# Chunks of 125 tokens, two chunks of edges per bucket and a joint stage without GpSimd in a graph transformer kernel

## The reference

```python
# L0: embedding, 4 hops over the graph, linear attention, 2 of 8 experts
xn = layernorm(x)
x1 = xn @ W1 + b1                       # 1250x512
out = x1
for k in range(4):
    deg = segment_sum(ones, dst); dis = maximum(deg, 1) ** -0.5
    alpha = tanh(out[dst] @ gw[k][:512] + out[src] @ gw[k][512:] + gb[k])
    out = out + segment_sum((dis[src] * dis[dst])[:, None] * alpha * out[src], dst)
x = x + concat([x1, out], 1) + attention0(xn) @ Wo.T + bo
x = x + experts(layernorm(x))           # the two best of 8 by a gate
# L1: a sparse linear layer built from the same edges, attention, gated MLP
xn = layernorm(x)
W = zeros(1024, 1024).at[row, col].add(nnz_weight)   # row=src, col=dst, edge_weight;
x = x + xn @ W.T + bias + attention1(xn) @ Wo1.T + bo1   # indices past 1023 are dropped
x = x + mlp(layernorm(x))
```

## Time and profile before

| | |
|---|---|
| median of 3 runs | 2728.61 us (2726.71 to 2731.57) |
| the profiled execution | 2738.93 us |
| its span | 2736.9 us |
| TensorE matmul | 2291.4 us (84%) |
| VectorE | 1724.4 us (63%) |
| ScalarE | 1007.2 us (37%) |
| GpSimd | 384.8 us (14%) |
| DMA, moved | 253.43 MB, 93 GB/s on average |

### The profile page before, as it was taken

The page is one execution under the profiler, slowest core; times in us unless marked ns, Lnnn a source line. Parts: engine busy times, 40 slices in busy tenths (PEclk is TensorE's granted clock), DMA queues, the critical chain, the costliest instruction groups (busy, mean ns, idle before and its releaser), DMA issues. The chain is left out here.

```text
span 2736.9 us, 33962 instructions
## 1 busy us (share of the span) xinstructions
PE 2291.4 (84%) x12790; PEld 2012.8 (74%) x12790; DVE 1724.4 (63%) x2712; ACT 1007.2 (37%) x1551; POOL 384.8 (14%) x332
## 2 busy tenths in 40 slices
PE   0689999994885699996279999994979999989798
PEld 0669999993663577775268888883759999977697
DVE  8865656656887877775279999995653333335422
ACT  0512322222442344441068888884112222221120
POOL 0257750002771000000200000001100000000000
PEclk9899999997998799996589999997999999999999
DMA  0252211103232000005655445514421111124314
GB/s 17 75 175 51 47 37 40 64 12 134 92 107 88 8 1 8 8 1 183 232 191 179 169 165 197 185 47 176 145 104 60 35 60 45 37 82 140 113 64 127
DMA packets 100988, 253.43 MB, mean 93 GB/s; under 512 B 16507, under 2 KB 43506, under 8 KB 100822
## 3 DMA queue, kind: packets, MB, share of 16 engines
q1 hardware_dynamic: 90006, 230.24, 24.0%
q0 software_dynamic: 10816, 20.99, 2.7%
HBM read 289.28 MB, written 81.27 MB: 135 GB/s over the span
## 5 line engine op out<-in xcount | busy, mean ns | idle before, releaser
L1945 DVE TENSOR_TENSOR ex_wl<-ex_raw,ex_wh 128x1024 fp32r<-128x1024 f32 x324 | 376.0, 1222 | 58.9 <-ACT ex_wh L2012 58.4
L2012 ACT ACTIVATE ex_wh<-ex_raw 128x1024 fp32r<-128x1024 f32 x324 | 329.6, 1059 | 94.3 <-DMA ex_raw<-in_experts 57.6
L1284 DVE TENSOR_TENSOR m_kvf<-m_bank,m_bkv 128x256 f32<-128x256 f32 (+1 forms) x160 | 67.9, 425 | 228.7 <-PE m_bank L1189 218.0
L953 POOL DMA_INDIRECT scratch_slots<-pay,idx x160 | 196.7, 1229 | 59.6 <-issue 59.6
L1434 PE MATMUL gl_bank<-gl_gh,gl_al 128*128 128x512 f32 (+3 forms) x400 | 164.6, 412 | 29.5 <-DVE g L1513 18.3
L1189 PE MATMUL m_bank<-m_w_lo,xh 128*128 128x256 f32 (+1 forms) x1280 | 178.4, 282 | 0.0
L1189 PE MATMUL m_bank<-m_w_hi,xl 128*128 128x256 f32 (+1 forms) x1280 | 177.5, 281 | 0.2 <-issue 0.2
L1189 PE MATMUL m_bank<-m_w_hi,xh 128*128 128x256 f32 (+1 forms) x1280 | 177.2, 281 | 0.0
L1189 PEld LDWEIGHTS m_bank<-m_w_lo,xh 128*128 128x128 f32 (+1 forms) x1280 | 163.9, 186 | 0.1
L1189 PEld LDWEIGHTS m_bank<-m_w_hi,xl 128*128 128x128 f32 (+1 forms) x1280 | 162.4, 186 | 0.6 <-issue 0.6
L1189 PEld LDWEIGHTS m_bank<-m_w_hi,xh 128*128 128x128 f32 (+1 forms) x1280 | 161.5, 186 | 0.2 <-issue 0.2
(11 more groups left out here) (396 smaller groups left out, 5527.2 us busy)
## 6 DMA issues: line engine op xcount, KB each, us to landing
ex_raw<-in_experts SPq DMA_DIRECT2D x324, 512.0 KB
m_w_raw<-in_qkv SPq DMA_DIRECT2D x48, 512.0 KB
ex_xr<-scratch_seats SPq DMA_DIRECT2D x27, 512.0 KB, 3.5
scratch_served<-ex_y SPq DMA_DIRECT2D x27, 512.0 KB, 2.6
scratch_at<-m_ats SPq DMA_DIRECT2D x48, 209.0 KB
o_ar<-scratch_at SPq DMA_DIRECT2D x18, 512.0 KB
o_xr<-scratch_res SPq DMA_DIRECT2D x18, 512.0 KB
scratch_res<-o_xr SPq DMA_DIRECT2D x18, 512.0 KB
```

Of the source, the lines that this page charges most:

```text
L953: e.indirect_dma_start(dram["slot_rows"], bass.IndirectOffsetOnAxis(idx[:, k:k + 1].bitcast(U32), 0), pay[:, k, :], None).then_inc(scat.se ...
L1284: e.tensor_tensor(f, bank[KVB + s % 3][0:r, 0:W2], bkv[0:r], ALU.add)
L1945: return e.tensor_tensor(wl[:, n % RING], raw[:, unit[1]], wh[:, n % RING].bitcast(F32), ALU.subtract)
L2012: e.activation(wh[:, n % RING], raw[:, unit[1]], ACT.Copy).then_inc(high.sem)
```

## The change

All chunks have `TP` = 125 tokens, ten of them. The chunk of an index is found by a multiplication with 1049 and a shift by 17. A bucket has two columns of 128 places (`HOME` = 2), so 200 columns of slots and not 300. In the given data a bucket holds 200 edges on average and 248 at most. The buckets are ordered by target first. `wmat` is a matrix of 1125x1125 in its natural layout, built from nine (`WB`) blocks each way.

```diff
-LAST = N - (TC - 1) * P
+TP = N // TC
-HOME = 3
+WB = -(-D // TP)
+HOME = 2
 def rows_of(c):
-    return P if c < TC - 1 else LAST
+    return TP
 def tokens(c):
-    return slice(c * P, c * P + rows_of(c))
+    return slice(c * TP, (c + 1) * TP)
```

In `graph_sort` the one-hot has 16-bit operands, four wide at the inside:

```diff
-            e.tensor_tensor(hot[:], key[:].unsqueeze(1).broadcast_to([EP, NBUCK, EK]),
-                            iob[0:EP, :].unsqueeze(2).broadcast_to([EP, NBUCK, EK]), ALU.is_equal)
+            by4 = lambda t: t.rearrange("p b (k f) -> p b k f", f=4)
+            e.tensor_tensor(by4(hot[:]), by4(keyb[:].unsqueeze(1).broadcast_to([EP, NBUCK, EK])),
+                            iob[0:EP].unsqueeze(2).broadcast_to([EP, NBUCK, EK // 4, 4]), ALU.is_equal)
```

```diff
         @block.gpsimd
-            e.wait_ge(*parted["wlo"])
-            for n, (i, q) in enumerate(groups):
-                if q == 0:
...
-                    e.tensor_tensor(t, t, bias[0:rows_of(i)], ALU.add).then_inc(based.sem)
-                if (i, q) in scaled.value:
...
-                    e.tensor_tensor(ws[:, r, HOME:HC, 0], hs[:, r, HOME:HC],
-                                    wide(whi[:, cut(i, q, HOME, HOME)].bitcast(F32), HOME), ALU.mult)
-                    e.tensor_tensor(ws[:, r, :, 1], hs[:, r], wide(wlo[:, cut(i, q)], HC),
-                                    ALU.mult).then_inc(scaled_pl.sem)
         @block.scalar
+            for n, (i, h) in enumerate(groups):
+                if h == 0 and i + 1 < TC:
+                    split_at(i + 1)
+                g = groups[n + 1] if n + 1 < len(groups) and groups[n + 1] in kept else None
+                if g:
+                    make_real(g)
+                note((i, h, 0))
+                if g:
+                    scale(g, 0, UN // 2)
+                note((i, h, 2))
+                if g:
+                    scale(g, UN // 2, UN)
+                note((i, h, 4))
         @block.vector
             def hot(n):
-                col = iot[:].unsqueeze(1).broadcast_to([P, HC, P])
-                e.tensor_tensor(hs[:, r], wide(slots[:, cut(i, q), 0], HC), col, ALU.is_equal).then_inc(source.sem)
-                e.tensor_tensor(hd[:, r], wide(slots[:, cut(i, q), 1], HC), col, ALU.is_equal).then_inc(target.sem)
+                by4 = lambda t: t.rearrange("p u (k f) -> p u k f", f=4)
+                col = by4(iot[:].unsqueeze(1).broadcast_to([P, UN, P]))
+                for t4, t, sem in ((s4, hs, source), (d4, hd, target)):
+                    val = t4[:, first(g):first(g) + UN].unsqueeze(2).broadcast_to([P, UN, P // 4, 4])
+                    e.tensor_tensor(by4(t[:, n % HOT]), col, val, ALU.is_equal).then_inc(sem.sem)
+            for n, (i, h) in enumerate(groups):
+                if h == 0 and i + 1 < TC:
+                    split_at(i + 1)
+                if n + 2 < len(groups):
+                    hot(n + 2)
+                if n + 1 < len(groups):
+                    low(n + 1)
+                add((i, h, 0))
+                if h == 0:
+                    rebase(i)
+                add((i, h, 2))
+                if h == 0 and i:
+                    evict(i - 1)
+                add((i, h, 4))
```

More of the change, by code:

```diff
@@ L525, in project_and_count @@
         x_out = [p.raises(f"x_out{b}", range(b, TC, 3), 16) for b in range(3)]
[L526 to L531, removed]
@@ L532, in project_and_count @@
-        stored = [p.raises(f"stored{b}", range(b, KC, 2), 16) for b in range(2)]
+        s_in, b_in, consts = p.raises("s_in", ["slots"], 16), p.raises("b_in", ["bias"], 16), p.raises("consts", ["iota"])
+        at_high, at_low, based, done, summed = (p.raises(n_, C) for n_ in ("at_high", "at_low", "based", "done", "summed"))
+        fours, parted = p.raises("fours", ["source", "target"]), p.raises("parted", ["wlo"])
+        source, target = p.raises("source", groups), p.raises("target", groups)
@@ L547, in project_and_count, with first @@
         block = p.block()
-        def cut(i, q, first=0, count=HC):
-            at_ = (i * TC + q * GW) * HOME + first
-            return slice(at_, at_ + count)
+        def first(g):
+            return (g[0] * TC + g[1] * HB) * HOME
         @block.sync
@@ L614, in _, with count @@
         @block.tensor
         def _(e):
-            def count(n):
-                g, b, r = groups[n], n % 2, n % RING
-                e.wait_ge(*cast[g])
+            def count(sub):
+                i, h, f = sub
+                g, n = (i, h), nth[sub]
+                b, r = n % 2, turn[g] % HOT
+                if f == 0:
+                    e.wait_ge(*target[g])
                 if n >= 2:
-                    e.wait_ge(*noted[groups[n - 2]])
-                for d in range(GW):
+                    e.wait_ge(*noted[subs[n - 2]])
+                for d in range(blocks(*sub, TC)):
@@ new lines, in scale, with note @@
+            def scale(g, from_, to):
+                n = kept[g]
+                for u in range(from_, to):
+                    c = first(g) + u
+                    a = e.activation(ws[:, n % EVEN, u, 0], hs[:, turn[g] % HOT, u, 0:TP], ACT.Copy,
+                                     scale=whi[:, c:c + 1].bitcast(F32))
+                if to == UN:
+                    a.then_inc(scaled.sem)
+            def note(sub):
+                i, h, f = sub
+                nb = blocks(*sub, TC)
+                e.wait_ge(*counted[sub])
+                e.activation(c16[0:TP, h * HB + f:h * HB + f + nb, tokens(i)], pc[nth[sub] % 2][0:TP, 0:nb, 0:TP],
@@ new lines, in _ @@
+            for u in range(4, KC):
+                w.make_high(e, u)
+            e.wait_ge(*parted["wlo"])
+            scale(groups[0], 0, UN)
+            for n, (i, h) in enumerate(groups):
[11 more added lines that the diff above has]
+                note((i, h, 4))
@@ L729, in _ @@
-            e.wait_ge(*ld["bias"])
+                e.tensor_tensor(t, t, py[c % 2][0:TP], ALU.add).then_inc(summed.sem)
+            e.wait_ge(*s_in["slots"])
             e.tensor_copy(whi[:], slots[:, :, 2])
@@ L1396, in _ @@
             for t in range(NT):
[L1397 removed]
+                m = e.matmul(bank[4 + t][:, 0:TW], ones[0:TP], ab[0:TP, tile(t)], start=True, stop=True)
             m.then_inc(row.sem)
```

342 lines of the change are left out of this document (180 added, 162 removed).

## The result

The changed kernel takes 2894.51 us (median of 4 runs, 2891.36 to 2898.59) against 2728.62 us: a ratio of 1.061, 95% interval 1.0597 to 1.0623. It is slower, as forecast, but by 166 us and not by 85, and the time lies outside the range of 2762 to 2852. The profiled execution took 2896.7 us with a span of 2895.0.

The account below looks back on a forecast made before the run. No engine bounds it throughout: waited-for transfers bound embedding, routing and the last stage; engines disturbing each other slow the joint stage. Terms -3+40-46+1.5+37+10+6+40 = +85.5 gave a median of 2814 us, range 2762 to 2852.

Parts of the forecast that it names:

- the transfer terms: All stages' added time from SyncE's 125-row tiles on five DMA engines: +134.5 us in all.
- The price of a 125-row transfer: SyncE's 125x1024 tile runs on 5 of 16 engines: 4.20 us against 1.34, so 2.86 more each.
- The first rival: 4 KB tiles spread over most engines, so transfer terms vanish: -49 us, 2680; chance 0.08.
- Transfers that GpSimd issues by an index list: GpSimd's indexed transfers were taken to be unlike SyncE's 125-row ones and costed at nothing.
- The last stage: Final load-and-store rounds grow from 5.55 to 10.6 us: +40 us (30 to 46).
- Embedding: Embedding's waiting rounds grow from 6.13 to 12 to 13.3 us, ending near 238: +40 us (28 to 46).
- Routing: Routing's six rounds grow from 5.6 to 9.9 to 11.3 us: +37 us (24 to 44).
- Serving: Three tiles now stand ahead of weights 4 to 7, plus a last store: +10 us (2 to 14).
- Joint stage: Weight-block period falls from 21.00 to 16.5 us, set by TensorE: -46 us (-33 to -56).
- The sort: Its 16000-element one-hot gets cheaper with 16-bit operands, less 1.2 for scalings and waits: -3 us (-7 to +1).
- The rest: Graph layer +1.5 (0 to 4), serving +10, second projection +6 (0 to 8), attention and experts 0.
- two rivals: Joint stage doesn't speed up, 2846 us, chance 0.13; half of embedding and routing is hidden, 2764, chance 0.10.

Follow-up runs that it names:

- the run with direct tiles on 16 engines: Changed kernel with SyncE's token tiles and sparse-weight block rows each moved as 112 and 13 rows; ratio 0.9909 to the kernel before.
- the kernel with both edits: Changed kernel with SyncE's tiles split into 112 and 13 rows and GpSimd's indexed tiles padded to 128 rows; 2663.60 us, ratio 0.9758 to the kernel before.

## Why the prediction was right and wrong

Over the whole kernel the sum splits so: giving the transfers their engines back is worth 231 us, where the transfer terms were 134.5; what is left of the change gains 65 us, where the sort and the joint stage were 49. That leaves 97 - 16 = 81 us, the distance from 85 to 166. Two steps failed: indexed transfers had no price, and the terms of the direct ones were too small, above all the joint stage's, which was nothing.

- **The price of a 125-row transfer: right.** Five engines, read from a DMA share of 0.33; the changed kernel shows 0.33 for a 4 KB tile (4.00 us, 112 GB/s), the cut into 96 and 29 rows shows the rule at its other end, and 112 and 13 rows take the price away. The first rival (4 KB rows spread over most engines, 2680) fell.
- **"Transfers that GpSimd issues by an index list are not of this kind and I cost them at nothing": the first of the two steps that failed.** The 40 of them in routing and serving cost 50 us. The changed kernel without this cost stands at a ratio of 1.0426, 2845 us on the first chip, which is inside the range. A sign was in the profile before, among GpSimd's groups, though it can be read only afterwards, since the transfers differ in bytes too: the edge scatters of 125 rows took 1229 ns each to issue and the indexed stores of 128 rows 955. In the changed kernel these take 1186. The groups of before, and of after:

```profile
L953 POOL DMA_INDIRECT scratch_slots<-pay,idx x160 | 196.7, 1229 | 59.6 <-issue 59.6
...
L1704 POOL DMA_INDIRECT scratch_seats<-ro_xn,seat x20 | 19.1, 955 | 83.6 <-DVE seat L1817 77.8 <-issue 5.8
```

```profile
L1760 POOL DMA_INDIRECT scratch_seats<-ro_xn,seat x20 | 23.7, 1186 | 128.9 <-DVE seat L1873 123.1 <-issue 5.8
```

- **The direct terms: 134.5 forecast, 201 measured by the stages (191 by the ratios): the second.** Taken from the run with direct tiles on 16 engines, what was missing is 19 us in the joint stage, 13 in the embedding, 12 in routing, 11 in serving, 7 in the last stage and 4 in the rest.
- **The last stage: right in kind, a little short.** Rounds of 11.04 us, near the upper of my two ends (11.3) and not the 10.6 between them: the fixed part stayed. The chain of waits is DMA for 82% of the stretch, as named; the share is 0.27 and not 0.31. +45.5 for +40, its upper bound 46.
- **Embedding: +53.4 for +40 (bound 46).** Rounds of 13.0 us where I had 12 to 13.3, but the tail was missing: the next phase begins at 245.2, when the last stores, issued from 230.0 on and sharing five engines, have landed. The stage ended 7 us later than the 238 named. (Its lower bound of +28 was a slip: 113.2 + 105 is 218, and 225 is 26.5 above 198.5.)
- **Routing: direct part +49.1 for +37, and the indexed 29 on top.** Six rounds of 10.87 us from 1273.48 to 1338.67; I took 10.5 and subtracted for a backlog.
- **Serving: +34.9 for +10 (bound 14).** 20.8 direct, 19.8 indexed, not quite additive. SyncE issues the first of weights 4 to 7 at 1962.28, 14.4 us after the phase's start at 1947.85, where it did so after 7.2 before (1885.13, 1877.93): the head had to wait for the first weights too, and I had counted only the three tiles ahead of the later ones. That the first weights are late because they share engines with a token tile and with the first gathers is likely, and not shown.
- **Joint stage: -41.5 for -46, a near hit by errors that cancel.** Its arithmetic gained 60.8 us. TensorE's period is 14.7 and not 16.4, because my price of a group took the whole time from 729.87 to 731.41, with its gaps, and scaled it by two thirds, 1.05. Without waits, in the kernel with both edits, four counts and four weight matmuls take 0.75 us:

```profile
713.25 0.39 PE L631 MATMUL o_pc<-o_hd,o_hs 128*125 128x125 bf16 x4
713.46 0.71 PE L645 MATMUL o_pw<-o_ws,o_hr 128*125 128x250 f32 x4
714.00 0.63 PE L229 MATMUL o_py<-o_w_lo,o_xh 128*125 128x512 f32 x2
```

  VectorE works about 12 us a chunk and not 16.1 (60.06 of 74), mostly because its 16-bit one-hots take 0.82 us and not 1.58. So the DMA became the bound, which I had put at 15.1, under 16.4, and which therefore had no term: it cost 19 us. Its 15.1 was itself added up wrong (10.5 is the embedding's sum, with a 512-column store that this stage doesn't have; two tiles and the weight's store make 13.0 by the same prices), and it had no fixed parts and no order. SyncE's rows show the order: the next load waits at 787.70 for the store issued at 775.08. The weight blocks' stores lie 17.3 us apart here, (793.69 - 759.04) / 2, two periods since short and long ones alternate. Over all eight intervals they lie 16.5 apart, (843.45 - 711.24) / 8, which is the number that I named, by luck: the first two are 13.3 and 14.7, before the tiles' transfers fall behind.

```profile
759.04 0.25 SPq L591 DMA_DIRECT2D scratch_wmat<-o_wacc  x1
...
775.08 0.40 SPq L594 DMA_DIRECT2D scratch_res<-o_xr  x1
787.70 0.25 SPq L574 DMA_DIRECT2D o_xr<-scratch_res  x1
...
793.69 0.25 SPq L591 DMA_DIRECT2D scratch_wmat<-o_wacc  x1
```

- **The sort: -6.7 for -3.** My nearest row, an operation of another kind at 0.79 ns an element, was too dear: the 16-bit one-hot takes 8.49 us, 0.53 ns an element. By the Trainium skill ("VectorE: DVE Perf Modes", "What auto-detection actually checks") an operation on two tensors makes two results a cycle where all operands are 16-bit and lie a step of one apart, from which I had estimated 8.4 us; the trace agrees.
- **The rest.** Graph layer +4.6 for +1.5, second projection +9.8 for +6: both over the upper end (4 and 8).

The range failed because it reached only 38 us above the forecast. It was drawn around two rivals and not around the terms: the direct ones alone came out 39 us over the sum of their upper bounds (201 for 162), and one kind of transfer had no term at all.

## What to carry to other kernels

A tile's row count decides how many DMA engines carry it: before a tiling is changed, factor the new row count, for the direct and for the indexed transfers. A full-looking DMA share doesn't clear an indexed transfer, since small packets add to it (68.5% for an estimated 41 of data); read the GB/s and the packets under 512 B beside it. A number of rows that suits arithmetic (125 = 1250/10) can be kept if each tile is moved as 112 + 13 rows, or an indexed one padded to 128. Where two gains and a loss meet in a stage, work out each resource's period without its waits, or the next bound comes out wrong.

## What the runs showed of the hardware

- SyncE's transfers ran on 5 engines for 125 rows (share 0.33 of 16), on 14 for 98 (0.88), and on 1 for 29 (0.06, 26 GB/s). A load and a store of 125 rows, both under way, got 111 GB/s together, and one alone 112.
- Indexed transfers of GpSimd with rows of 4 KB fit the same divisors (120 as fast as 128; two gathers of 127 rows on two engines, share 0.13 and 52 GB/s, costing 61 us over 16 gathers). The packet counts fit one small packet per row of a working engine for each engine left out: 272, 368 and 1904 more packets for 125, 124 and 127 rows.
- A VectorE comparison of two 16-bit tensors took 0.64 ns an element (0.82 us for 1280), with float32 operands 1.16 (1.48 us); in a stretch where GpSimd was busy for half of the time the 16-bit one took 1.65 and 1.82 us on average, for 0.82.
